# The second expert layer's preparation moved into the attention before it, in one block, with the gate as the stationary operand of the logits

## The reference

```python
x = x + _L0_xattn_ref(_layernorm(x, axis=-1), ctx_1024, ...)
x = x + _L0_ffn_ref(_layernorm(x, axis=-1), gate_w, expert_bias, w1, w2)
x = x + _L1_xattn_ref(_layernorm(x, axis=-1), ctx_1024, mask, Wq, Wkv, Wo)
x = x + _L1_ffn_ref(_layernorm(x, axis=-1), Wg, alpha, ln_w, ln_b, fc1_w, fc1_b, fc2_w, fc2_b)
```

```python
logits = xf @ Wg
top_vals, top_idx = jax.lax.top_k(logits, TOP_K)
gate_score = jax.nn.softmax(top_vals, axis=-1)
comb = jnp.einsum('tke,tk->te', one_hot, gate_score) * alpha
for e in range(Wg.shape[1]):
    hdn = _layernorm(xf, ln_w[e], ln_b[e])
    a = jax.nn.gelu(hdn @ fc1_w[e] + fc1_b[e], approximate=True)
    y = a @ fc2_w[e] + fc2_b[e]
    out = out + y * comb[:, e:e + 1]
```

## Time and profile before

| what | us |
|---|---|
| median of 3 runs (960.53 to 969.27) | 964.39 |
| the profiled execution | 967.79 |
| its span, first to last instruction | 965.9 |
| PE busy in it | 894.5 (93%) |
| granted PE clock over it | 0.956 |

### The profile page before, as it was taken

The page is one execution under the profiler, slowest core; times in us unless marked ns, Lnnn a source line. Parts: engine busy times, 40 slices in busy tenths (PEclk is TensorE's granted clock), DMA queues, the critical chain, the costliest instruction groups (busy, mean ns, idle before and its releaser), DMA issues. The chain is left out here.

```text
span 965.9 us, 19473 instructions
## 1 busy us (share of the span) xinstructions
PE 894.5 (93%) x6189; PEld 766.2 (79%) x6190; DVE 562.0 (58%) x1286; ACT 491.3 (51%) x1044; POOL 431.3 (45%) x374
## 2 busy tenths in 40 slices
PE   6899999868999998779999999988899999999995
PEld 4798989746899996557777777757499999999995
DVE  7875453485566675666566575554764454454452
ACT  5744141354444553475665665545655455455552
POOL 2474341004555573755363462300255555555543
PEclk9999999978999999789999999985999999999998
DMA  9721000275766746611010100019667666676662
GB/s 306 239 95 44 1 1 1 76 248 187 254 228 232 253 157 221 135 44 44 5 63 22 45 1 2 28 52 353 229 184 195 211 200 190 209 203 187 206 198 28
DMA packets 68593, 134.72 MB, mean 139 GB/s; under 512 B 8080, under 2 KB 50704, under 8 KB 63408
## 3 DMA queue, kind: packets, MB, share of 16 engines
q1 hardware_dynamic: 55184, 110.27, 33.4%
q0 software_dynamic: 13344, 23.63, 11.2%
HBM read 109.08 MB, written 21.64 MB: 135 GB/s over the span
## 5 line engine op out<-in xcount | busy, mean ns | idle before, releaser
L1901 PEld LDWEIGHTS d_hps<-d_xg_t,d_xw 128*128 128x128 f32 x1248 | 145.2, 192 | 2.4 <-DVE d_xg_t L2085 1.0
L1799 ACT ACTIVATE x<-d_hps,b 128x128 f32<-128x128 f32 x312 | 89.3, 368 | 113.1 <-PE d_hps L1901 112.9
L1901 PE MATMUL d_hps<-d_xg_t,d_xw 128*128 128x128 f32 x1248 | 145.5, 275 | 0.8 <-DVE d_xg_t L2085 0.8
L883 POOL TENSOR_SCALAR c_prob<-c_prob,c_rinv 128x1024 f32<-128x1024 f32 x64 | 72.4, 1150 | 109.4 <-DVE c_rinv L1338 109.0
L1911 PE MATMUL d_yps<-d_w,d_hid_hi 128*128 x312 | 115.2, 402 | 0.0
L1704 POOL DMA_INDIRECT out_x<-d_y,d_take_slot x39 | 63.1, 1619 | 99.1 <-DVE d_y L2122 89.6
L1331 DVE CUSTOM_DVE_ANT_0 c_prob<-c_sc,c_minf 128x1024 f32<-128x1024 f32 x64 | 75.8, 1221 | 36.6 <-PE c_sc L976 34.4
L2085 DVE TENSOR_SCALAR d_xg_t<-d_take,ln_w,ln_b 128x128 f32<-128x128 f32 x78 | 28.5, 406 | 93.4 <-PE d_take L1890 93.1
L1914 PE MATMUL d_yps<-d_w,d_hid_lo 128*128 x312 | 81.2, 281 | 0.0
L1901 PEld LDWEIGHTS b_hps<-b_xg_t,b_w 128*128 128x128 f32 x624 | 76.7, 195 | 3.6 <-issue 1.9
L989 PE MATMUL c_tp<-const,c_prob 128*128 128x128 f32 x512 | 70.5, 281 | 9.8 <-DVE c_pt L1343 5.2
(11 more groups left out here) (367 smaller groups left out, 2106.6 us busy)
## 6 DMA issues: line engine op xcount, KB each, us to landing
d_xw<-in_w SPq DMA_DIRECT2D x39, 1024.0 KB
b_w<-in_w SPq DMA_DIRECT2D x47, 512.0 KB, 7.6
d_w<-in_w SPq DMA_DIRECT2D x8, 1024.0 KB, 12.3
a_raw<-in_ctx_t SPq DMA_DIRECT2D x8, 512.0 KB, 7.0
a_raw<-in_ctx SPq DMA_DIRECT2D x8, 512.0 KB, 4.6
ybuf<-a_zero SPq DMA_DIRECT2D x2, 2048.0 KB, 12.5
k_stage<-in_ctx_t SPq DMA_DIRECT2D x12, 256.0 KB, 3.0
rows<-b_xn_all SPq DMA_DIRECT2D x1, 2048.0 KB, 12.6
```

What stands on the lines that cost most here:

```text
L883: nc.gpsimd.tensor_scalar(prob[w][:], prob[w][:], rinv[:, w:w + 1], 1.0, ALU.mult, ALU.mult).then_inc(s["prob_ready"], 1)
L1799: op = nc.scalar.activation(hid[q][:, h * FH + c, :], src[:, c, :], ACT.Gelu_apprx_tanh, bias=b1[:, ds(e, 1), h * FH + c])
L1901: mm = nc.tensor.matmul(hps[j % 2][h][:, c * P:(c + 1) * P], w1[j % WL][:, k, at:at + P], xg_t[j % 2][:, k, :], start=(k == 0), stop=(k == ...
```

## The change

The second experts are built before the attention, at the bottom of SBUF, and all three programs stand in one block, so that no meeting of the engines lies between the attention and the second experts. The second experts' preparation is spread over the attention:

- w2 of experts 2 and 3 (`EARLY_LOW`) is loaded in batch 1, and its halves are split by ACT after units 1 and 7 of batches 1 and 2 (`HIGH_AFTER`) and by DVE after units 2, 2, 3 and 2 of batches 1, 2, 2 and 3 (`LOW_AFTER`). w2 of experts 0 and 1 (`LATER_LOW`) is loaded when the last values are projected; ACT splits both and DVE one of them between the last pieces of the attention. Expert 4 is loaded after the last maximum, 5 to 7 after the last product with the values.
- The root for the first three batches moves ahead of the last head copies on ACT, and DVE normalises their twelve tiles between its last attention pieces (`early_normal`). SP writes these twelve tiles to DRAM at once (`early_rows`), the last four and `b2` behind them. The last batch's statistics are taken in two halves (`half_stats`) behind the two additions.
- In both expert layers the logits have the gate as stationary operand: two matmuls of 256 moving columns a pair into a bank of `low`, so that a group of four tiles stands there by expert. ACT copies each group to SBUF (`keep_logits`) and PE turns it back with four small transposes (`turn_logits`). The warm-up matmul behind each pair goes, and in the second experts also the five ahead.
- `PE_LOW` has two experts in the second layer, none after the sums of `take_slot`; `DVE_LOW` is experts 1 and 4, `DVE_LAST` is expert 5. Several semaphores become counts of one (`routed`, `act_routed`, `pe_routed`).

```diff
+EARLY_LOW = (2, 3)
+LATER_LOW = (0, 1)
+FREE_FIRST = 4
+LAST_LOW = (5, 6, 7)
...
@@ attention1, sync @@
                 if b > 1:
                     out_rows(b - 2)
+                else:
+                    sp.wait_ge(s["sum_p"], 2 * TB * (B - 1))
+                    for n in EARLY_LOW:
+                        m.load_w2(sp, n)
+            sp.wait_ge(s["v_done"], B * 4)
+            for n in LATER_LOW:
+                m.load_w2(sp, n)
             out_rows(B - 2)
             sp.dma_start(dram["out"][T * P:(T + 1) * P, :], m.x[:, 0, :]).then_inc(m.out_ready, 16)
+            sp.wait_ge(s["max_done"], B * UP * 2)
+            m.load_w2(sp, FREE_FIRST)
+            m.early_rows(sp)
+            sp.wait_ge(s["av_done"], B * 4)
+            for n in LAST_LOW:
+                m.load_w2(sp, n)
             out_rows(B - 1)
...
@@ attention1, scalar @@
+        HIGH_AFTER = ((1, 1), (1, 7), (2, 1), (2, 7))
                 keep_first(b, 0, 1)
+                if (b, 1) in HIGH_AFTER:
+                    m.early_high(act, HIGH_AFTER.index((b, 1)))
...
             keep_first(B - 1, 7, 0)
+            root(0, B - 1, 21)
             keep_heads(B - 1, 2)
             keep_first(B - 1, 7, 1)
+            for n in LATER_LOW:
+                m.high(act, n)
             keep_heads(B - 1, 3)
-            root(0, B - 1, 21)
...
@@ attention1, vector @@
+        LOW_AFTER = ((1, 2), (2, 2), (2, 3), (3, 2))
+            def half_stats(half):
+                dve.wait_ge(s["x_ready"], B * 2 - 1 + half)
+                for t in range(T - TB + 2 * half, T - TB + 2 * half + 2):
+                    op = nc.vector.bn_stats(m.bn[:, t, :], m.x[:, t, :])
+                op.then_inc(s["x_bn"], 1)
...
-            keep_second(B - 1, 7, 0)
-            keep_second(B - 1, 7, 1)
             dve.wait_ge(s["x_bn"], 2 * B - 1)
             variance(nc, m, dve, s["stat"], cols(0, B - 1), 15)
-            late_scale(0, B - 1, 15, 3)
+            keep_second(B - 1, 7, 0)
+            dve.wait_ge(s["v_done"], B * 4)
+            inverse_std(nc, m, dve, s["stat"], s["sqrt_done"], cols(0, B - 1), 15, 3)
+            m.early_normal(dve, 0, 5)
+            keep_second(B - 1, 7, 1)
             add_projection(B - 1, 0, xb)
+            m.early_normal(dve, 5, T - TB)
+            half_stats(0)
+            m.later_low(dve, LATER_LOW[0])
             add_projection(B - 1, 1, tp[1])
+            half_stats(1)
...
@@ experts @@
-    DVE_LOW, PE_LOW, DVE_LAST = ((0, 1, 2, 3), (4, 5), (6, 7)) if first else ((0, 1), (2, 3, 4), (5, 6, 7))
-    HIGH_AT = (1, 3, 5, 7) if first else (3, 5)
-    LOW_LATE = PE_LOW[len(PE_LOW):] if first else PE_LOW[-1:]
+    DVE_LOW, PE_LOW, DVE_LAST = ((0, 1, 2, 3), (4, 5), (6, 7)) if first else ((LATER_LOW[1], 4), (6, 7), (5,))
+    HIGH_AT = (1, 3, 5, 7) if first else (2, 5)
...
+        def early_high(act, n):
+            e, cs = half_of(n)
+            act.wait_ge(w2_in[e], 16)
+            nc.scalar.activation(w2[:, e, cs, 0, :], w2[:, e, cs, 1, :].bitcast(F32), ACT.Copy).then_inc(s["w2_half"], 1)
+
+        def early_normal(dve, lo, hi):
+            for t in range(lo, hi):
+                normalise(nc, m, xn_all[:, t, :], t).then_inc(s["xn_dve"], 1)
+
+        def early_rows(sp):
...
+            sp.wait_ge(s["xn_dve"], T - TB)
+            sp.dma_start(dram["rows"][0:(T - TB) * P, :].rearrange("(t p) d -> p t d", p=P),
+                         xn_all[:, 0:T - TB, :]).then_inc(s["xn_out"], 16)
...
+            def keep_logits(group):
+                act.wait_ge(s["logit_done"], 2 * group + 2)
+                nc.scalar.activation(by_expert[:, group * 4 * P:(group + 1) * 4 * P], logit_t(group),
+                                     ACT.Copy).then_inc(s["logit_kept"], 1)
...
             def logits(i):
+                group, at = i // 2, i % 2 * 2 * P
                 pe.wait_ge(s["xn_t"], i + 1)
-                for a in range(2):
-                    t = 2 * i + a
-                    for k in range(KD):
-                        mm = nc.tensor.matmul(lps[:, t * ne:(t + 1) * ne], xn_t[i % TPX][:, a, k, :], gw[:, k, :],
-                                              start=(k == 0), stop=(k == KD - 1))
+                if i % 2 == 0 and group >= 2:
+                    pe.wait_ge(s["logit_kept"], group - 1)
+                for k in range(KD):
+                    mm = nc.tensor.matmul(logit_t(group)[:, at:at + 2 * P], gw[:, k, :], xn_t[i % TPX][:, :, k, :],
+                                          start=(k == 0), stop=(k == KD - 1))
                 mm.then_inc(s["logit_done"], 1)
+
+            def turn_logits(group):
+                pe.wait_ge(s["logit_kept"], group + 1)
+                for a in range(4):
+                    t = 4 * group + a
+                    mm = nc.tensor.transpose(lps[:, t * ne:(t + 1) * ne], by_expert[:, t * P:(t + 1) * P], ident[0:ne, 0:ne])
+                mm.then_inc(s["pe_routed"], 1)
...
-            warm(5, rank)
+            if first:
+                warm(5, rank)
...
                 logits(i)
-                warm(1, rank)
+                if i % 2 == 0 and i:
+                    turn_logits(i // 2 - 1)
+            turn_logits(PAIRS // 2 - 1)
```

More of the change, by code:

```diff
@@ L33 @@
 LANES = 3
+EARLY_LOW = (2, 3)
+LATER_LOW = (0, 1)
+FREE_FIRST = 4
+LAST_LOW = (5, 6, 7)
+ROUTED = {n: k + 1 for k, n in enumerate("load exp_in expert blk val slot g gate_at".split())}
+ACT_ROUTED = {n: k + 1 for k, n in enumerate("exp_ready val0_ready off_ready lane_act".split())}
+HIGH_ORDER = (0, 1, 4, 5, 6, 7)
 GATHERS = 6
@@ L741, in attention1 @@
         wq_hi, wq_lo = (a[:, 6, :].rearrange("p (k d) -> p k d", k=KD) for a in (m.split_hi, m.split_lo))
+        y_late = [[sb(f"y{b}_{k}", [P, TB, D]) for k in range(2)] for b in (2, 3)]
+        sb("gap", [P, 5248])
         q_hi, q_lo = (sb(f"q_{p}", [P, KD, S], F32R) for p in ("hi", "lo"))
@@ L748, in attention1 @@
         att_odd = sb("att_odd", [P, 2 * P])
-        y_late = [[sb(f"y{b}_{k}", [P, TB, D]) for k in range(2)] for b in (2, 3)]
-        sb("gap", [P, 5248])
         wo = sb("wo", [P, KD, D])
@@ L1443, in vector @@
                 keep_second(b, 4, 1)
+                if not more:
+                    new_stats(b - 1)
                 both_maxima(b, 6)
@@ L1501, in experts @@
         c16 = lambda at, n: m.c16[:, at - C_ONES:at - C_ONES + n]
+        if not first:
+            xw = sb("xw", [P, T * D])
         w2 = sb("w2", [P, E, FC, 2, D], F32R)
@@ L1611, in flat_part, with load_w2, high, high_count @@
             return tile[:, ds(part, 1), :].rearrange("p a j -> p (a j)")
+        def load_w2(sp, e):
+            sp.dma_start(w2[:, e, :, 1, :].bitcast(F32),
+                         dram[f"w2_{layer}"][e].rearrange("(c p) d -> p c d", p=P)).then_inc(w2_in[e], 16)
+        def high(act, e):
+            act.wait_ge(w2_in[e], 16)
+            nc.scalar.activation(w2[:, e, :, 0, :], w2[:, e, :, 1, :].bitcast(F32), ACT.Copy).then_inc(s["w2_hi"], 1)
+        def high_count(e):
+            return e + 1 if first else HIGH_ORDER.index(e) + 1
@@ L1613, in run @@
+        if not first:
+            m.load_w2, m.high, m.early_high, m.early_low, m.later_low = load_w2, high, early_high, early_low, later_low
+            m.early_normal, m.early_rows = early_normal, early_rows
         def run(eng, step):
@@ L2213, in build, with _ @@
-        with nc.cleanup_on_exit():
-            last = experts(nc, m, dram, 1)
-            with nc.Block() as block:
-                block.sync(last.sync)
-                block.tensor(last.tensor)
-                block.scalar(last.scalar)
-                block.vector(last.vector)
-                block.gpsimd(last.gpsimd)
+            with nc.Block() as block:
+                @block.sync
+                def _(sp):
+                    first.sync(sp)
+                    second.sync(sp)
+                    last.sync(sp)
+                @block.tensor
+                def _(pe):
+                    first.tensor(pe)
+                    second.tensor(pe)
+                    last.tensor(pe)
+                @block.scalar
+                def _(act):
+                    first.scalar(act)
+                    second.scalar(act)
+                    last.scalar(act)
+                @block.vector
+                def _(dve):
+                    first.vector(dve)
+                    second.vector(dve)
+                    last.vector(dve)
+                @block.gpsimd
+                def _(pool):
+                    first.gpsimd(pool)
+                    second.gpsimd(pool)
+                    last.gpsimd(pool)
```

241 lines of the change are left out of this document (124 added, 117 removed).

## The result

The changed kernel takes 957.4 us (median of 17 runs, 954.2 to 960.2), the kernel before 962.1 beside it (17 runs, 957.5 to 969.3). The ratio is 0.9935, its interval 0.9916 to 0.9955: faster by 0.65%. That is clear of the noise, but under one per cent, so by the prediction's classes it counts as the same, which had a chance of 0.36 there. The time lies 4.9 us above the forecast of 952.5, inside its range. The profiled execution of the changed kernel took 955.69 us; the forecast for it was 955.9. So the sum holds from profile to profile and not from median to median. The experiments ask why.

The account below looks back on a forecast made before the run. PE was taken to bound the second attention and experts, but not the 55.8 us preparation between. Gains 11.7 + 3.3 less 1.4 and 1.7 make 11.9: profiled 967.8 becomes 955.9, or 952.5 against the median 964.4; range 945 to 962.

Parts of the forecast that it names:

- the prediction's classes: Whole kernel, with one per cent (9.6 us) as border: faster 0.59, the same 0.36, slower 0.05.
- From the attention's end to the routing: Second experts' preparation, last projection to routing: 15.3 us in place of 27.0, a gain of 11.7.
- a pair's pitch: Second experts' logits: each pair takes 1.36 us at full clock, eight pairs and four groups 12.5 us.
- ACT's two high parts: Second experts' logits: 1.90 us each ahead of copies PE waits for; cost 1.9, bounds 0 and 3.8.
- the second rival: Second experts' logits: clock falls to 0.50, the stretch takes 25.9 us, time 963.1; chance 0.08.
- the third: Second experts: w2 of expert 5 lands late, ACT holds the last two pairs 3.5 us more, time 956.0; chance 0.15.
- the rule that the forecast cited: Second experts' logits: transposes don't count as work for the clock; only wide logits, 0.92 of each 1.36 us, would hold it.
- From the rows known to the first up: Second experts: 5.6 us against 8.9, a gain of 3.3, bounds 0 and 4.
- The first ups: Second experts: first up takes 5.00 us against 3.57, a loss of 1.4, from 0 to 3 for both first ups.
- The first experts: First experts' logits: a pair takes 1.56 us instead of 1.44 and the last copy adds 0.7, a loss of 1.7.
- its upper bound: First experts' logits: a loss of 3.4 us if all four copies of 0.6 on ACT show.
- The attention: Inside the attention: nothing added; PE loses up to 2 us in all if cover is gone, never a gain.

Follow-up runs that it names:

- e6: Changed kernel with the second experts' high parts of experts 4 and 5 put behind the low parts: 955.1 us, 0.9942 of the kernel before.
- e5: Kernel before with the stationary gate alone, in both layers, still two blocks: 965.1 us, 1.0044 of the kernel before.
- e1: Kernel before run and profiled again with no edit: 961.6 us, ratio 1.0003; its profiled execution took 960.9 us.
- e4: Changed kernel with the old logits (gate moving) in the first experts alone: 955.7 us, 0.9947 of the kernel before.
- e7: Changed kernel with gate moving in both layers and second experts' high parts of experts 4 and 5 behind the low parts: 951.5 us, 0.9897 of before.
- e8: Changed kernel with 20 (second experts) and 22 (first) warm-up matmuls instead of 8 before the first gathered rows: 952.7 us, 0.9911 of before.
- e11: Changed kernel with late high parts of experts 4 and 5 and 20 or 22 warm-ups before the gathered rows: 952.7 us, 0.9886 of before.

## Why the prediction was right, and where it was wrong

**From the attention's end to the routing.** Forecast 15.3 us behind the projection, measured 15.0 (645.43 to 660.40), a gain of 12.0 against the first profile (forecast 11.7). Inside, two sizes were off and cancelled: a pair's pitch is 1.54 (646.68 to 648.22), not 1.36, which is 1.4 over eight pairs, and ACT's two high parts cost 0.8 (e6), not 1.9. The clock held, and the second rival didn't come. Nor did the third: ACT's row at 654.50 has no idle time before it. With the stationary gate the clock was 1.00 through these logits in all eight profiles, in e5 even behind the idle gap at the border. That doesn't speak against the rule that the forecast cited, since the wide matmuls stand between the transposes.

**From the rows known to the first up.** Forecast 5.6, measured 5.6. **The first ups:** forecast a loss of 1.4, measured 1.1 in the second experts (8.5 for 7.4). In the first experts it takes 5.87, for 5.00 in the first profile, but 5.86 in e1, so nothing there is the change's. **The first experts:** forecast 1.7, measured 2.0 to the routing (16.6 from the block's start for 14.6). The way is the one given for its upper bound, ACT: with the second copies in its FIFO the fourth high part comes at 198.02, DVE waits 2.22 us for it, and the fourth low part ends as the routing starts. **The attention:** nothing forecast, 1.0 more in this pair of profiles and 1.0 less against e1, which is what runs differ by. That the profiled execution came within 0.2 us of its forecast is luck in part: 1.5 of its gain lies ahead of the first experts (183.76 for 185.30), where the change does nothing, and about as much was lost in the attention and behind the first down.

**The step that failed** is the sum's last: "The profiled execution's own 967.8 becomes 955.9. It lies 3.4 above the median of the runs, 964.4, and against that the forecast is 952.5." It takes the whole gain of 11.9 off a run that never had the whole loss. In an execution at the median (e1) the stretch to the routing is 19.8 us, not 29.0, and the change gains 2.9 there. Against e1 the account is 2.9 to the routing, 5.7 to the first up, less 2.5 in the first experts and 1.2 in the first up, and 0.2 more in the rest: 5.1, the difference of the spans (959.0 and 953.9) and about that of the medians, 4.7. The largest term there is the stretch from the rows known to the first up, 11.3 us in e1. The prediction gave it 3.3, for PE's third low part and its warm-ups; in e1 they end 1.2 us ahead of the gathered rows, and what ends last is the rows, which no longer stand behind the weight loads. The chance of 0.59 for faster by over 1% came from the same wrong step.

"TensorE: Matmul & The Clock Gate" of the Trainium skill, in "What's actually happening", says of a kernel's start that the number of matmuls at the low clock varies between runs of one kernel, and puts the cost of that ramp under 1% of a typical kernel's span. The stretch here lies in the middle of the kernel, and its size agrees: 6.9 of 965.9 us is 0.7%, and it was more than the whole effect of the change.

**What stays open:** what decides the draw, and why runs at 0.960 or less are 10 of 39, 6 of 34 and 7 of 11 on the three chips; what e4's four slower runs are; how much of the 5.7 is owed to the early rows and how much to the third low part that is gone.

## What to carry to other kernels

Before a term is taken from a stretch at the low clock, compare the profiled run's time and mean clock with the other runs': where the slow profile lies in the tail, work the sum for both clocks, and look in each for what ends last. A second profile of the unchanged kernel at the median would have more than halved this forecast's gain. Of a change with several parts, time each alone: here one part paid some 9 us, another cost 4; with it in two blocks twelve runs had no low draw, but in one block the moving gate in both layers had none either, so nothing that it bought there is shown.

## What the runs showed of the hardware

- The granted clock of the same instructions, PE busy 5.00 of 5 us, was 0.50 in one execution and 1.00 in another (655 to 660 in the two profiles of the kernel before); in e7 it fell between two groups of logits with no idle time in the rows around them.
- Four fp32 matmuls with eight moving columns (eight records) took 0.95 us in e7, two with 256 columns (four records) 1.03 in the changed kernel: at the full clock the narrow form, which needs no second copy, is as cheap.
- Twenty warm-up matmuls over 4.02 us and a gap of one us kept the clock for the next 64 records in e8 (7.31 us) and not in e11 (8.77).
- A gathered block took 2.74 us from issue to landing with 0.20 of the DMA engines' time in use (680 to 685 in the changed kernel), and 8.04 in e1, beside two loads of 1 MB.
